# Two FFN tiles more ahead of the choice of experts, one split ahead of its weights, and eight widenings done as transposes

## What is computed

```python
o, new_state = _gla_scan(qh * dk ** (-0.5), kh, vh, gkh)
o = o + jax.nn.sigmoid(aug_w[..., None] * vh)
mu = o.mean(-1, keepdims=True)
var = o.var(-1, keepdims=True)
o = (o - mu) * lax.rsqrt(var + EPS)
...
out = jax.nn.silu(g) * o @ Wout
```

```python
logits = jnp.einsum('bsd,ed->bse', hidden_states, gate_w) + gate_b
scores = jax.nn.softmax(logits, axis=-1)
top_v, top_i = jax.lax.top_k(scores, TOP_K)
val_sum = top_v.sum(axis=-1)
for e in range(E):
    count = (top_i == e).sum(axis=-1).astype(hidden_states.dtype)
    gate = count * val_sum
    inter = einsum(hidden_states, wi) + bi + einsum(einsum(hidden_states, lora_A[e]), lora_B[e])
    h = jax.nn.relu(inter)
    expert_out = jnp.einsum('bsf,df->bsd', h, wo) + bo
    out = out + gate[..., None] * expert_out
```

## Time and profile before

| | |
|---|---|
| Runs (3) | 1330.08, 1330.54, 1335.51 us; median 1330.54 |
| Profiled execution | 1326.59 us; its span 1325.3 us; mean granted clock 0.976 |
| TensorE busy | 1238.9 us, 93% |
| VectorE busy | 731.3 us, 55% |
| ScalarE busy | 517.4 us, 39% |
| GpSimd busy | 137.7 us, 10% |
| TensorE's idle time behind VectorE's z | 5.2 us, in two waits |

### The profile page before, as it was taken

The page is one execution under the profiler, slowest core; times in us unless marked ns, Lnnn a source line. Parts: engine busy times, 40 slices in busy tenths (PEclk is TensorE's granted clock), DMA queues, the critical chain, the costliest instruction groups (busy, mean ns, idle before and its releaser), DMA issues. The chain is left out here.

```text
span 1325.3 us, 25936 instructions
## 1 busy us (share of the span) xinstructions
PE 1238.9 (93%) x11101; PEld 925.3 (70%) x11101; DVE 731.3 (55%) x1572; ACT 517.4 (39%) x1018; POOL 137.7 (10%) x158
## 2 busy tenths in 40 slices
PE   6999889979587999999999999999899889999999
PEld 4565468856344777777777777777688758887887
DVE  4468486546597455555545455555585745434432
ACT  3234447422013255444545445454453422222321
POOL 2300021234431300000000000000031100000000
PEclk9999999989888999999999999999999989999999
DMA  9659600000211410111000000000400200000200
GB/s 287 253 206 399 225 0 1 0 1 1 70 65 53 155 65 34 35 46 50 33 33 34 34 33 34 33 34 33 82 1 1 73 0 32 32 32 32 64 32 32
DMA packets 49334, 88.23 MB, mean 67 GB/s; under 512 B 19210, under 2 KB 20284, under 8 KB 45124
## 3 DMA queue, kind: packets, MB, share of 16 engines
q1 hardware_dynamic: 48160, 86.01, 18.9%
q10 hardware_dynamic: 1060, 0.56, 0.2%
HBM read 65.59 MB, written 20.97 MB: 65 GB/s over the span
## 5 line engine op out<-in xcount | busy, mean ns | idle before, releaser
L1856 ACT ACTIVATE K<-bank,vecT 128x512 f32<-128x512 f32 x64 | 44.1, 689 | 171.5 <-PE bank L256 171.5
L1871 ACT ACTIVATE W<-W,low 128x512 f32<-128x512 f32 x128 | 90.9, 712 | 46.7 <-DVE low L1775 46.7
L186 POOL TENSOR_TENSOR rstd<-rstd,half_pow 128x1 f32<-128x1 f32 x48 | 29.9, 628 | 706.2 <-DVE rstd L182 706.2
L1775 DVE CUSTOM_DVE_ANT_0 W<-bank,W 128x512 f32<-128x512 f32 x128 | 80.8, 687 | 40.0 <-PE bank L1644 40.0
L1753 DVE TENSOR_TENSOR W<-bank,vecT 128x256 f32<-128x256 f32 x16 | 6.8, 425 | 166.0 <-PE bank L1665 166.0
L256 PE MATMUL bank<-xT,wT 128*128 128x512 f32 x384 | 96.1, 399 | 0.0
L256 PE MATMUL bank<-woT,hR 128*128 128x512 f32 x384 | 93.2, 398 | 2.2 <-DVE hR L273 2.2
L256 PE MATMUL bank<-Wq,Wkv 128*128 128x512 f32 x384 | 93.0, 394 | 0.0
L256 PE MATMUL bank<-Wkv,ctxT 128*128 128x512 f32 x384 | 92.9, 395 | 0.0
L256 PE MATMUL bank<-ctxT,Wkv 128*128 128x512 f32 x384 | 92.6, 394 | 0.4 <-DVE ctxT L273 0.4
L256 PE MATMUL bank<-Wkv,Wq 128*128 128x512 f32 x384 | 92.4, 395 | 0.0
(11 more groups left out here) (350 smaller groups left out, 2243.2 us busy)
## 6 DMA issues: line engine op xcount, KB each, us to landing
W<-ctx_turned SPq DMA_DIRECT2D x16, 1024.0 KB, 4.8
W<-in_ctx_dram SPq DMA_DIRECT2D x8, 1024.0 KB, 10.3
ctx_turned<-ctxT SPq DMA_DIRECT2D x8, 1024.0 KB, 7.4
ctx_turned<-W SPq DMA_DIRECT2D x8, 1024.0 KB, 6.5
XT<-in_ctx_dram SPq DMA_DIRECT2D x4, 1024.0 KB, 11.7
XT<-in_L_ffn_wi_dram SPq DMA_DIRECT2D x4, 1024.0 KB, 6.1
XT<-in_L_ffn_wo_dram SPq DMA_DIRECT2D x4, 1024.0 KB, 5.0
raw_own<-in_ctx_dram SPq DMA_DIRECT2D x3, 1024.0 KB, 11.3
```

Source lines behind the costliest of these rows:

```text
L186: pool.tensor_tensor(rstd[:, g:g + 1], rstd[:, g:g + 1], half_pow[:], ALU.pow).then_inc(rstd_ok.s, 1)
L1775: dve.tensor_tensor_reduce(out=PR[:, j, :], in0=bank[:, 4 + j % 4, :], in1=mask, scale=1.0, scalar=3.0e38, op0=ALU.add, op1=ALU.min, accum ...
L1856: act.activation(K[:, m, :], bank[:, n % 4, :], ACT.Identity, bias=pcol("L1_xattn_bk", m)).then_inc(ring_a.s, 1)
L1871: act.activation(PR[:, j, :], PR[:, j, :], ACT.Exp, bias=low[:, j:j + 1], scale=-1.0, accum_out=total[:, j:j + 1]).then_inc(expd.s, 1)
```

## The change

1. In gated attention, `widen_pe` calls TensorE's transpose on `wide` where it called a matmul with the identity.
2. In the mixture, the hidden products of tiles 2 and 3 are issued right after the second pair of picks, ahead of all that needs z; the later tiles keep their places.
3. At the start of the last product, ScalarE and VectorE split hR of w = 0 before woT of f = 0 (in before, after it), and TensorE's wait for the last tile's join stands ahead of the third of the four groups of rows, whose banks 2 and 3 the tiles use, where it stood ahead of the first.

```diff
                 for t in range(C):
-                    ins = pe.matmul(bank[:, 6, t * P:(t + 1) * P], wide[:, t * P:(t + 1) * P], ident[:], start=True, stop=True)
+                    ins = pe.transpose(bank[:, 6, t * P:(t + 1) * P], wide[:, t * P:(t + 1) * P], ident[:])
                 ins.then_inc(wide_pe.s, 1)
...
                 pe.wait_ge(wt_v.s, wt_v(2 + FT + f))
-                if w == 0:
-                    pe.wait_ge(joined.s, joined(N2 * FT - 1))
                 for g in range(4):
+                    if w == 0 and g == 2:
+                        pe.wait_ge(joined.s, joined(N2 * FT - 1))
...
                 pick_chosen_pe(1)
+                for u in (2, 3):
+                    hidden_pe(*tiles[u], u)
                 for u in range(len(tiles) + 1):
                     if u < len(tiles):
-                        if u >= 2:
+                        if u >= 4:
                             hidden_pe(*tiles[u], u)
                         expert_pe(*tiles[u], u)
...
-                        if w < FT:
+                        if 0 < w < FT:
                             turn_weight_v(FT + w)
                         n, f = w // FT, w % FT
                         dve.wait_ge(hr_a.s, hr_a(w))
                         split_v(hR[:, w % 2, 1, :], hid(f, n), hR[:, w % 2, 0, :]).then_inc(hr_v.s, 1)
+                        if w == 0:
+                            turn_weight_v(FT)
...
-                    if w < FT:
+                    if 0 < w < FT:
                         turn_weight_a(FT + w)
                     act.wait_ge(joined.s, joined(f * N2 + n))
                     if w >= 2:
                         act.wait_ge(prod.s, produced(w - 2))
                     split_a(hR[:, w % 2, 0, :], hid(f, n)).then_inc(hr_a.s, 1)
+                    if w == 0:
+                        turn_weight_a(FT)
```

## The result

The changed kernel takes 1316.68 us (median of 4 runs, 1313.18 to 1318.26) against 1333.03 (4 runs, 1330.08 to 1336.76): ratio 0.9872, 95% interval 0.9836 to 0.9909. Forecast was a ratio of 0.9915 (11.3 us) and 1319.2 us. The profiled execution took 1313.18, its span is 1311.9 us, 13.4 less than before. Two single runs lay more than 1.5% above the fastest of their kernel (one of 67 of before, one of 27 of the change) and are called slow: medians and ranges keep them, ratios and means leave them out.

The account below looks back on a forecast made before the run. TensorE, busy 93% of the span, was taken as the bound, so less work in full stretches or filled idle ones pays. 7.58 + 0 + 3.75 = 11.3 us off 1330.54 gives 1319.2 us, range 1314.5 to 1324.5.

Parts of the forecast that it names:

- Part 1: Mixture, picks to hidden product of tile 4: moving tiles 2 and 3 ahead of z gains 7.58 us, bounds 2.6 to 8.8.
- The chain: Mixture after the second picks: TensorE's order followed through pick copy, z, relus and joins, tile 4 starting at 1091.55, not 1099.13.
- what is late next: Mixture, before hidden product of tile 4: join, relu, turned weight make TensorE late by 0.5 us, once.
- The rival of a clock that falls here in spite of it: Mixture: clock falls despite shorter waits, costing 5 us, 1324.2; chance 0.14 together with a fall before the last product.
- Part 2: Start of last product: swapping the splits gives 0, both staying queued on VectorE; ends 2.23 us gain, 0.6 loss.
- Part 3: Gated attention's widening by transposes: 3.75 us gained over eight calls; ends 5.0 and 0.
- 0.63 us of TensorE: Gated loop: saving per widening call, 0.99 us for eight matmuls less 0.36 for four transposes.
- Call 5: Gated loop's widening call without scores between: mean product stands right behind ScalarE's copy, so gain 0.
- the end of the loop: Calls 6 and 7 of the widening: VectorE's addition before the multiply leaves 0.3 us each, 0.6 together.
- The sum: Whole change: 7.58 + 0 + 3.75 = 11.3 us less, 1319.2 us; chance 0.62.
- The rival of a newly fallen clock before the last product: Clock newly falls in the 2.23 us wait, costing 5 us, 1324.2; chance 0.14 together with a fall in the mixture.
- The rival of transposes that let the clock fall in the loop: Gated loop: a period at low clock lasts 7.8 us more; one gives 1327.0, two 1334.8, five 1358; chance 0.06.

Follow-up runs that it names:

- e2_tiles: Only the hidden products of tiles 2 and 3 moved ahead of z, against the kernel before: 1326.76 us (12 runs), ratio 0.9958.
- e5_one_tile: The whole change with only tile 2 ahead of z, tile 3 in its old place: 1333.05 us (one run), picks to tile 4 16.63 us.
- e3_split: Only the last product's edits (hR split ahead of its weights, later wait for the last join), against the kernel before: 1330.69 us, ratio 0.9988.
- e8_early_split: The whole change plus the last product's first operands split before the relus of the last tiles: 1316.12 us (6 runs), ratio 0.9865 to before.
- e1_transposes: Only the widening's matmuls with the identity replaced by transposes, against the kernel before: 1332.23 us (12 runs), ratio 0.999.
- e6_widen4: The whole change with each widening's four transposes issued four times: loop period 10.20 us against 8.89, clock 1.00; 1325.69 us (one run).

## Why the prediction was right

**Part 1, 7.58 us forecast, 7.21 measured.** From the picks to tile 4 there are 13.2 us in every profile with this part, and 19.8 to 20.5 in the four with the old order. The chain held link by link: the start behind ScalarE's pick copy, no wait for z, and the turned weight as what is late next. The missing 0.4 us are small: the pair of hidden products started 0.05 later and took 0.09 longer than twice 2.80, the relu of tile 0 came 0.05 and its second product 0.17 later than added up. (In the prediction 1086.4 + 0.69 was put at 1087.2; it is 1087.1, so the sum was 0.1 too cautious there.) Of the 7.21 us, 4.4 are waiting (5.15 us before, 0.77 after) and 2.8 matmuls that no longer run at the low clock, where the prediction had some 3.5 for it. e2_tiles and e5_one_tile show the cause, waits and clock together. The rival of a clock that falls here in spite of it did not occur in seven profiles with both tiles ahead.

**Part 2, 0 forecast, 0 measured** (e3_split 0.9988, wait 2.32 instead of 2.23). The reason held: two splits behind the last join on VectorE, whichever is first. e8_early_split shows the other side: once they are ahead of the relus, the wait goes to 0.70.

**Part 3, 3.75 us forecast, about 3.1 added up from the profiles, 3.1 of work in the runs.** The term that was mis-sized is the saving per call, "0.63 us of TensorE": it is 0.46, and so the distance from L999 to L962 is 0.53 us where the prediction had 0.36 to 0.45, and the period 8.89 where it had 8.7. I took the 0.36 us of four transposes between two long products; among the loop's short matmuls a group of four takes 0.53, which is four times 0.109 and 0.09 once. So 5 x 0.46 = 2.3. Call 5 gave 0.06 where I had put 0, and the end of the loop 0.70 where I had 0.6. Why transposes between long products stand closer (0.09 us apart) was not tried.

**The sum was partly lucky.** Both terms came out smaller than forecast, 7.2 + 3.1 = 10.3 us by the profiles. That the means of all runs give 11.6, next to 11.3, is within their error of 1.2 and does not confirm the tenths.

**The clock.** The rival of a newly fallen clock before the last product was in the forecast with 0.14, and it was there in the profile of the change. Nothing shows it to be the change's: with a wait of 2.2 to 2.3 us it fell in 5 of 10 profiles, in 2 of the 4 that leave this place as in before (e1_transposes, e2_tiles) and in 3 of the 6 with the new order. The rival of transposes that let the clock fall in the loop is refuted by e6_widen4. The Trainium skill's sentence that the full clock does not engage for transposes (TensorE: Matmul & The Clock Gate, Part 4: PE-mode transpose) is not what the traces show, here nor in the earlier trace rows.

**The surplus** of the first comparison, 16.4 instead of 11.3 us, did not come back: the two later comparisons give 0.9907 and 0.9924, and no part holds it. The first profiles put 3.5 us of it before the changed stretch; three profiles of the changed kernel have the first L962 at 262.4, 265.9 and 269.2 us, so a difference of this size comes and goes there without any change.

## What to carry to other kernels

A wait of TensorE is worth more than its length when the clock falls behind it: here 4.4 us less of waiting became 7.2 us of time. Before moving an operand ahead of another, look at what its engine still has queued in front of both; swapping the last two of a queue changed only the releaser's name here. Read the cost of a short group as the distance of starts among neighbours like those it will have, and time differences under 0.5% with span times granted clock beside the median.

## What the runs showed of the hardware

- A plain 128x128 f32 product is two recorded matmuls and a transpose of the same size one, at 0.11 us each: 0.53 against 0.99 us for four.
- After the waits of 2.5 us and more for z the clock fell in all five profiles that have one; in e1_transposes it was low only from the second wait on. At the loop's start, behind a wait of 2.6 us for the masks, it fell in all twelve profiles: L978's eight matmuls take 1.7 to 2.1 us there and 1.16 later, as in the changed kernel:

```profile
266.18 1.21 PE L975 MATMUL bank<-Am,V 128*32 128x128 f32 x32 [2.60 <-DVE Am L1141]
267.32 2.08 PE L978 MATMUL bank<-ident,XT 128*128 128x128 f32 x8
...
275.66 1.16 PE L978 MATMUL bank<-ident,XT 128*128 128x128 f32 x8
```

- After 2.2 to 2.3 us before the last product it fell in 5 of 10 profiles; behind the 2.2 us of standing at the mixture's start it was low in 8 of 12. After 0.7 us and less, at the picks and before the last product, it fell in none.
- With nothing but transposes on TensorE at the mixture's start the clock rises, but not at once: by 1052 in before, where they begin at 1047.5, and in the changed kernel, where they begin at 1038.5, it is still low in the stretch below and at 1.00 from 1046 on. There, too, TensorE had done only transposes up to 1046.5:

```profile
1043.00:1045.00 2.00, 2.00 (x12) 2.00 (x11) 1.85 (x4) 1.47 (x3) 1.33 (x5) 0.50 1.01 379
```
